# First attention of a two-layer gated cross-attention kernel: guard and copy dropped, query projection and output projection moved on TensorE

## What is computed

```
x = x + tanh(g_xattn[0]) * L0_xattn(layernorm(x), ctx, ctx)   # 16 heads of 16, 77 keys: the first attention
x = x + tanh(g_ffn[0])   * L0_ffn(layernorm(x))               # gelu(x @ patterns), mean, top-k, ...
x = x + tanh(g_xattn[1]) * L1_xattn(layernorm(x), ctx, ctx)   # with rotary positions and a mask
x = x + tanh(g_ffn[1])   * L1_ffn(layernorm(x))               # 16 experts and a shared one

L0_xattn:  q = x Wq^T + bq;  k, v likewise from ctx
           attn = softmax(-0.25 * q k^T);  out = (attn v) Wp^T + bp
```

## Time and profile before

| | |
|---|---|
| time, 3 runs | 737.0 us median (736.0 to 739.29) |
| the profiled execution | 738.46 us, its span 736.7 us |
| busy over the span | TensorE 655.6 us (89%), VectorE 454.4 (62%), ScalarE 353.8 (48%), GpSimd 237.6 (32%) |
| chain of work that ended last | TensorE 71%, VectorE 15%, issue 5%, DMA 3% |
| first attention | iteration 0 about 31 to 46 us, iterations 1 to 5 to 102 us, 6 and 7 to about 127 us |

### The profile page before, as it was taken

How to read it: one execution, slowest core, us unless ns; L and a number is a source line. 1 busy time by engine, 2 the same in 40 slices (tenths; PEclk the granted TensorE clock), 3 DMA queues, 4 the chain that set the end, 5 groups by cost and what they waited for, 6 DMA issues and landing times.

```text
span 736.7 us, 13204 instructions
## 1 busy us (share of the span) xinstructions
PE 655.6 (89%) x4816; PEld 534.0 (72%) x4816; DVE 454.4 (62%) x944; ACT 353.8 (48%) x780; POOL 237.6 (32%) x250
## 2 busy tenths in 40 slices
PE   4898988899988777766999979999888999999998
PEld 3676665778866455544566657999877999999997
DVE  3779877110117476767787636548896877778703
ACT  3267656656652233241657675233276565655400
POOL 6644522600000410036775312000134455555400
PEclk9899999999999989995999999999999999999999
DMA  7856650592000053005767642200002566666313
GB/s 260 266 159 159 184 149 1 214 420 83 0 0 1 15 205 106 7 1 133 143 157 138 144 68 85 88 2 1 1 0 86 178 210 204 203 203 203 114 29 114
DMA packets 61348, 87.17 MB, mean 118 GB/s; under 512 B 17257, under 2 KB 50665, under 8 KB 60265
## 3 DMA queue, kind: packets, MB, share of 16 engines
q1 hardware_dynamic: 60496, 85.90, 38.8%
q10 hardware_dynamic: 800, 0.59, 0.3%
HBM read 63.54 MB, written 18.73 MB: 112 GB/s over the span
## 4 chain that ended last, share of the span: by engine, by line
PE 71%; DVE 15%; issue 5%; DMA 3%; ACT 3%; POOL 2%; ACTq 0%; DVEq 0%; POOLq 0%
PE ps L1093 69%; DVE keep L2030 2%; DMA m_rows<-big 1%; DMA keep<-in_x 1%; DVE keep L2041 1%; PE ps L1099 1%; DVE keep L2038 1%; DVE keep L2023 1%; DVE G L2243 1%; ACT vp L768 1%; DVE mcol L1838 1%; DVE hhi_s L2170 1%; DVE att L2168 0%; ACT ps L889 0%; DVE keep L1852 0%
## 5 line engine op out<-in xcount | busy, mean ns | idle before, releaser
L1093 PE MATMUL ps<-keep 128*128 128x120 bf16 (+7 forms) x473 | 60.6, 257 | 20.0 <-DVE keep L2030 14.7
L1093 PE MATMUL ps<-thi,whi 128*128 128x256 f32 x256 | 73.6, 287 | 4.1 <-POOL tlo L698 2.1
L1093 PE MATMUL ps<-thi,wlo 128*128 128x256 f32 x256 | 72.3, 283 | 0.0
L1093 PE MATMUL ps<-tlo,whi 128*128 128x256 f32 x256 | 72.2, 282 | 0.0
L1093 PEld LDWEIGHTS ps<-keep 128*128 128x128 bf16 (+1 forms) x473 | 34.1, 112 | 41.2 <-DVE keep L2030 26.2
L889 ACT ACTIVATE ps<-ps 128x256 f32<-128x256 f32 x128 | 47.6, 372 | 33.8 <-PE ps L1093 33.7
L1001 ACT ACTIVATE att<-ps 128x512 f32<-128x512 f32 x48 | 28.6, 596 | 65.6 <-PE ps L1093 65.4
L562 POOL TENSOR_TENSOR kbr<-khi,keep 128x616 fp32r<-128x616 f32 x32 | 39.8, 1265 | 61.2 <-PE ps L1093 59.0
L1093 PE MATMUL ps<-xhi,phi 128*128 128x512 f32 x128 | 51.5, 402 | 5.3 <-ACT ps L889 2.9
L1093 PEld LDWEIGHTS ps<-thi,whi 128*128 128x128 f32 x256 | 48.6, 190 | 6.0 <-issue 3.6
L1093 PE MATMUL ps<-xhi,plo 128*128 128x512 f32 x128 | 50.6, 395 | 0.0
(11 more groups left out here) (250 smaller groups left out, 1854.9 us busy)
## 6 DMA issues: line engine op xcount, KB each, us to landing
q_rows<-qhi SPq DMA_DIRECT2D x32, 256.0 KB, 2.7
big<-in_piw SPq DMA_DIRECT2D x4, 2048.0 KB, 13.4
qpair<-q_rows SPq DMA_DIRECT2D x8, 768.0 KB, 5.7
qhead<-q_rows SPq DMA_DIRECT2D x8, 768.0 KB, 7.7
q_rows<-qlo SPq DMA_DIRECT2D x16, 256.0 KB, 2.9
att<-in_wg SPq DMA_DIRECT2D x8, 512.0 KB, 3.7
att<-in_wu SPq DMA_DIRECT2D x8, 512.0 KB, 4.6
att<-in_wd SPq DMA_DIRECT2D x8, 512.0 KB, 5.6
```

The costliest lines, as they stand in the source:

```text
L1093: return pe.matmul(out, lhsT, rhs, start=start, stop=stop, skip_group_check=True)
```

## The change

In the first attention:

- TensorE: the query projection of block n + 2 stands at the head of iteration n, ahead of the first key scores. Its first row scores follow behind these, then the output projection of block n - 1, and only then the second key scores. Second row scores come before the third key scores.
- ScalarE: the high queries are taken before the first exponentials, and the second normalisation moves from behind the third exponentials to before the second.
- VectorE: the guard is gone, and the reciprocal reads the denominators where they are. The second statistics move from behind to before the second half of the maxima.

In both attentions the aggregation writes `fmv` directly, without the copy, and GpSimd waits for the two aggregations. The counts of the semaphore within `divide` go from three steps to two.

```diff
@@ attend, ScalarE @@
+                    if n + 2 < hi and layer == 0:
+                        high_queries(n + 2)
                     exponentials(n, (0, 1))
                     if n == 2 * B - 1:
                         round_shared(0)
-                    if n + 2 < hi and layer == 0:
-                        high_queries(n + 2)
...
+                    if n >= 2 and layer == 0:
+                        normalise_second(n - 2)
                     exponentials(n, (2, 3))
...
-                    if n - 2 >= lo:
+                    if n - 2 >= lo and layer == 1:
                         normalise_second(n - 2)
@@ attend, TensorE @@
+                    if m < hi and layer == 0:
+                        project_q(m)
                     key_scores(n, (0, 1))
-                    if m < hi:
-                        if layer == 0:
-                            project_q(m)
-                        else:
-                            swap_pairs(m)
+                    if m < hi and layer == 1:
+                        swap_pairs(m)
...
+                    if layer == 0 and m < hi:
+                        if m >= 5:
+                            pe.wait_ge(xlo_done, m - 4)
+                        first_rows(m)
+                        if n > lo:
+                            project_out(n - 1)
                     key_scores(n, (2, 3))
                     if layer == 0 and m >= hi:
                         early_acts(m - hi, 1)
-                    if layer == 0:
-                        if m < hi:
-                            if m >= 5:
-                                pe.wait_ge(xlo_done, m - 4)
-                            first_rows(m)
-                    elif n + 3 < hi:
+                    if layer == 1 and n + 3 < hi:
                         scale_rows(n + 3)
...
+                    if m < hi and layer == 0:
+                        second_rows(m)
                     key_scores(n, (4, 5))
-                    if n > lo:
+                    if n > lo and (m >= hi or layer == 1):
                         project_out(n - 1)
-                    if m < hi:
-                        if layer == 0:
-                            second_rows(m)
-                        else:
-                            first_rows(m)
+                    if m < hi and layer == 1:
+                        first_rows(m)
@@ stats_second, VectorE @@
-                    dve.bn_aggr(fag[:, t, :], fbn[:, t, :]).then_inc(faggr_done, 1)
-                dve.wait_ge(faggr_done, k * 2 + 2)
-                dve.tensor_copy(fmv[:, tiles(b), :], fag).then_inc(fmv_done, 1)
+                    dve.bn_aggr(fmv[:, 2 * b + t, :], fbn[:, t, :]).then_inc(fmv_done, 1)
@@ divide, VectorE @@
-                dve.tensor_scalar(den, turned4[:, :, :, HD], TINY, None, ALU.max).then_inc(div_step, 1)
-                dve.wait_ge(div_step, 3 * i + 1)
-                dve.reciprocal(rec, den).then_inc(div_step, 1)
+                dve.reciprocal(rec, turned4[:, :, :, HD]).then_inc(div_step, 1)
@@ attend_first, VectorE @@
                     if n > 0:
                         add_projection(n - 1)
+                        stats_second(n - 1)
                     if n + 2 < B:
                         maxima(n + 2, 1)
-                    if n > 0:
-                        stats_second(n - 1)
                     divide(n, 0)
@@ inv_std_second, GpSimd @@
-                pool.wait_ge(fmv_done, k + 1)
+                pool.wait_ge(fmv_done, 2 * k + 2)
```

More of the change, by code:

```diff
@@ L111, in flamingo_kernel @@
         fbn = keep(2 * 6).rearrange("p (t k) -> p t k", k=6)
-        fag = keep(2 * 2).rearrange("p (t k) -> p t k", k=2)
         fmv = keep(T // P * 2).rearrange("p (t k) -> p t k", k=2)
@@ L125, in flamingo_kernel @@
         scaled = tk[:, 512:768]
-        den, rec = (tk[:, at:at + 16].rearrange("p (a t) -> p a t", a=2) for at in (768, 784))
+        rec = tk[:, 768:784].rearrange("p (a t) -> p a t", a=2)
         tied, above, above_lo, eqb = (keep(64).bitcast(BF16) for _ in range(4))
@@ L267, in flamingo_kernel @@
         cleared, prepared, tanh_done, bpt_done = sem("cleared"), sem("prepared"), sem("tanh_done"), sem("bpt_done")
-        fstat_done, faggr_done, fmv_done = sem("fstat_done"), sem("faggr_done"), sem("fmv_done")
+        fstat_done, fmv_done = sem("fstat_done"), sem("fmv_done")
         fveps_done, frstd_done = sem("fveps_done"), sem("frstd_done")
@@ L1845, in divide @@
                 if n >= B:
-                    dve.wait_ge(div_step, 3 * 2 * B + i - 2 * B + 1)
+                    dve.wait_ge(div_step, 2 * 2 * B + i - 2 * B + 1)
                     dve.wait_ge(proj_ps, n)
@@ L1853, in divide @@
                 dve.wait_ge(half_read, i + 1)
-                dve.tensor_scalar(den, turned4[:, :, :, HD], TINY, None, ALU.max).then_inc(div_step, 1)
-                dve.wait_ge(div_step, 3 * i + 1)
-                dve.reciprocal(rec, den).then_inc(div_step, 1)
-                dve.wait_ge(div_step, 3 * i + 2)
+                dve.reciprocal(rec, turned4[:, :, :, HD]).then_inc(div_step, 1)
+                dve.wait_ge(div_step, 2 * i + 1)
                 dve.tensor_tensor(scaled.rearrange("p (t a d) -> p a t d", a=2, d=HD), turned4[:, :, :, 0:HD],
                                   rec.unsqueeze(3).to_broadcast([P, 2, S // 32, HD]), ALU.mult).then_inc(div_step, 1)
-                dve.wait_ge(div_step, 3 * i + 3)
+                dve.wait_ge(div_step, 2 * i + 2)
                 if n > 0:
```

## The result

The changed kernel takes 734.4 us, the median of 20 runs (731.03 to 738.79), and the kernel before beside it 741.11 us, the median of 20 (735.27 to 746.78): ratio 0.9908, 95% interval 0.9884 to 0.9932. So the change saves some 0.6 to 0.9%, 4.5 to 6.8 us, where the forecast had 4.6 us. The forecast's 732.4 us started from three runs of before at 737.0; the twenty beside the changed kernel lie 4.1 us higher, which is why the time came out 2.0 us above the forecast although the gain is larger.

The account below looks back on a forecast made before the run. The prediction saw one loop through three engines, TensorE and VectorE about equally full, decided by who waits for whom. Terms 3.0 - 1.1 + 1.07 + 1.64 = 4.6 us gave profiled 733.8, median 732.4 us; range 729.0 to 736.3.

Parts of the forecast that it names:

- Step 1: Iteration 0: query projection fills TensorE's wait for the maxima and the clock stays at 2.4 GHz; gain 3.0 us.
- ScalarE's queue end: Iteration 0: ScalarE's queue ends later than TensorE's 42.0, so iteration 1 starts at 42.6 us.
- Step 2: Iterations 1 to 4: the new order takes 47.25 us against 46.17; loss 1.1 us.
- VectorE has slack here, and its 0.59 us is hidden: Iterations 1 to 4: the 0.59 us taken off VectorE saves nothing, being hidden by TensorE's two waits.
- VectorE was the real limit: Rival, iterations 1 to 4: VectorE sets the loop, some 11.3 us an iteration, gain 1.0, total 730.3 us; chance 0.15.
- delays the maxima: Iterations 1 to 4: statistics moved ahead delay the second maxima by 0.94 us, still ending at 9.05, before TensorE's 9.5.
- Step 3: Into iteration 6: the early pattern matmuls come 12.8 us after iteration 5's start, against 13.87; gain 1.07 us.
- Step 4: Iterations 6 and 7: clock stays up (1.05 us) and VectorE drops two guards and a copy; gain 1.64 us.
- the clock falls all the same: Rival: clock still falls at 30 and 105 us, leaving gain 2.3, 734.7 us, no measurable change; chance 0.20.
- The port: Rival, iterations 1 to 3: GpSimd's work meets VectorE's products on SBUF, 1.8 us lost, 734.2 us; chance 0.14.
- The guard at 81.83: Iteration 4: guard took 0.75 us instead of 0.17, ending with GpSimd's key blocks; taken as agreeing with the exclusion rule.
- Slower: Rival: clock falls inside the loop, about 3.2 us each time; three falls cost 9.6, total 742.0 us; chance 0.06.

Follow-up runs that it names:

- e12: The changed kernel, unchanged, run and profiled again beside the kernel before on one chip: 736.34 us, ratio to before 0.9940.
- e9: Kernel before without guard and copy on VectorE, second statistics moved ahead of the second maxima, other orders old: 739.85 us, ratio to before 0.9975.
- e8: Kernel before without guard and copy, iteration 0's query projection and high queries moved first, other orders old: 734.08 us, ratio to before 0.9904.
- e2: Changed kernel with guard and copy put back on VectorE, so the new orders alone: 741.05 us, ratio to before 1.0002.
- e4: Kernel before with only iteration 0's query projection and high queries moved first: 741.6 us, ratio to before 0.9988.
- e5: Changed kernel with the second key scores ahead of the output projection again: 736.72 us, ratio to before 0.9937.
- e6: e5 with ScalarE's normalisation of four blocks ahead moved before the second exponentials in iterations 1 to 3: 736.51 us, ratio to before 0.9950.
- e13: The program of e8, unchanged, run and profiled again: 735.40 us, ratio to before 0.9934.
- e10: e8 with VectorE splitting the pattern tile and making the low part before its first division in iteration 5: 731.06 us, ratio to before 0.9866.
- e11: The kernel before, unchanged, run and profiled again: 739.98 us, ratio to before 0.9987.
- e3: Changed kernel with iteration 0's query projection and high queries back in the old order: 735.88 us, ratio to before 0.9937.
- e1: Kernel before without guard and copy on VectorE, every order as before: 736.01 us against 742.48, ratio 0.9921.

## Why the prediction was right, step by step

The forecast was 4.6 us. By the stages the change saves 90.81 - 85.26 = 5.55 us, 5.61 in the second pair of profiles, and the runs, 4.5 and 6.8 us, lie around it. In the first pair 1.67 of this did not show at O, because A came late.

**Step 1, iteration 0: 3.0 forecast, 3.5 measured.** From A to the start of iteration 1 were 16.99 us (28.61 to 45.60) and are 13.48. e12 starts iteration 1 at 41.83, the forecast had 42.6. The forecast had ScalarE's queue end too late, and that was the mis-sized term: ScalarE does hold TensorE (0.74 us at 42.76), but the iteration still ended half a microsecond sooner than taken. The size hangs on the clock: e9, in the old order but at a clock of 1.00 from 30 to 37 us, takes 14.48 from A to P1, and e8, which has only the order of iteration 0 different up to there, 13.70. So without the fall the order is worth about 0.8. Over all profiles the clock stayed at 1.00 in iteration 0 in all nine with the query projection first (after, e12, e2, e4, e5, e6, e8, e13, e10) and fell in four of the five with the old order (before, e11, e3, e1, but not e9).

**Step 2, iterations 1 to 4: 1.1 lost by the forecast, 0.55 measured.** The output projection came 4.00 after the start (3.89), and the starts of e12 lie 11.49, 11.77, 11.75 and 11.69 apart (11.7, 11.95, 11.95 and 11.65): ScalarE's copy of the maxima holds the next projection up by 0.23 and not 0.3. The sign was right. Wrong was "VectorE has slack here, and its 0.59 us is hidden": the maxima were to end at 9.05, 0.45 ahead of TensorE's 9.5, and they end at 9.22, 0.07 ahead of the transposes at 9.29. With guard and copy back in, the loop takes 0.95 longer (e2, 47.67), because its maxima are then too late for the transposes. And the old loop was VectorE's, but for 0.69 us in which it waits for the output projection: without these 0.59 us it takes 43.85. The rival *VectorE was the real limit* was thus true of the kernel before, and false of the changed one, because the statistics ahead of the maxima (3.9 us by e9) give back more than VectorE had gained. The forecast saw that this "delays the maxima" and costed it at nothing.

**Step 3, into iteration 6: 1.07 forecast, 0.88 measured.** From the end of the maxima to the pattern matmul it is 3.77 us (3.75 forecast), but the maxima end 9.22 after the start and not 9.05. The gap shrank from 2.43 to 0.91 us as forecast.

**Step 4: 1.64 forecast, 1.71 measured (13.78 to 12.07).** Both parts came as forecast. From E to the addition at 108.06 are 4.59 us, 1.15 less than before (1.05 forecast), and from there to O 7.48, 0.56 less (0.59 forecast). That the first part is the clock show e8 and e13, one program: with the fall it takes 5.99 us (100.55 to 106.54), without it 4.59 (98.88 to 103.47), and the rest up to O is 7.46 in both.

The rivals: *the clock falls all the same* came true in e2 behind a gap of 1.60 us (E to O 13.96) but in neither profile of the changed kernel. *The port* came in part: five products took longer than 0.5 us (0.54 to 0.82), and soon after four of them VectorE stood 0.72 to 0.83 us waiting for another engine, so they cost the loop nothing. The fifth, at 100.64, lies in the chain to the pattern matmul and took 0.66 us where before's took 0.43. GpSimd's work beside the longest, the product at 77.20:

```profile
76.52 1.23 POOL L561 TENSOR_TENSOR kbr<-khi,keep 128x616 fp32r<-128x616 f32 x1
77.70 1.41 POOL L561 TENSOR_TENSOR kbr<-khi,keep 128x616 fp32r<-128x616 f32 x1
```

The first ended at 77.75 and the product at 78.02, 0.27 behind it; the second took 1.41 us where these instructions take 1.22 in the median, so both engines slowed. The Trainium skill (SBUF — State Buffer, "two separate sides") has the two exclude each other for a whole instruction. The rows agree with that: the product ended only behind GpSimd's first, and GpSimd's second was the one that got longer. The guard at 81.83, which the forecast counted as agreeing, reads one tile only and is no test of the rule as the forecast put it. *Slower* did not come: the clock was 1.00 from 44 to 100 us.

So the gain came out right for mostly the right reasons, with one of them upside down. By the stages the dropped steps alone give 4.2 us (e1, in a profile without the fall behind E) and the order of iteration 0 alone 3.9 (e4); both together give 8.3 (e13), and the rest of the new order takes 2.7 of that back. The forecast had the steps worth nothing in the loop and everything there down to TensorE's waits. The total did not suffer from that, because the forecast added up the new loop as a whole and not the two halves of the change.

## What to carry to other kernels

When a loop runs through several engines, take each dropped instruction out alone: a saving that the new order hides may be the full pace of the old one. Ahead of a result that another engine waits for, put nothing that nobody waits for; one group of statistics in front of the maxima cost 1 us in every iteration. Judge changes of under 1% by stages between fixed points of the trace, and where the stages and the whole time disagree, as for e4, e10 and e13, say so.

## What was not expected of the hardware

The whole time of one program moves by over 1% with the granted clock (735.28 to 745.46 us for before). Yet in both profiles of one program most falls stand at the same places, and a few do not. Behind O, e11 falls where before does and once more, 415 us behind O. The two profiles of the changed kernel agree up to 235 us behind O, and e12 then falls at three places more, 240, 325 and 450 us behind O. The second of these, first in the changed kernel's first profile, then in e12:

```profile
440.50:445.50 5.00, 5.00 (x75) 3.12 (x73) 3.27 (x9) 2.74 (x6) 2.13 (x4) 1.00 0.00 0
438.50:443.50 5.00, 4.49 (x13) 3.50 (x14) 1.22 (x1) 3.94 (x7) 0.00 (x0) 0.50 0.00 0
```

A gap in TensorE's work ahead of the first pattern matmul of 2.43 us had a fall behind it three times out of three (before, e11, e4), 2.06 us once in three (e8, but not e1 and e13), 1.60 us in the one profile that has it (e2; so had the 1.49 us of e10 at the output projection), 1.31 us once in three (e9, but not e5 and e6), and 0.9 us in none of three (after, e12, e3). In iteration 0 a gap of 1.38 to 1.40 us had one three times out of three (before, e11, e3) and 2.89 us in e1, but 1.31 (e9) and 1.32 us (e2) had none. So a short wait costs its own length and, by chance, 1.4 us more (e8 against e13).

Left untried: the changed kernel's order on TensorE with the maxima ahead of the statistics on VectorE, which by e9 should be the shortest loop, and longer series of e10 and e13, which could settle their last 0.3%.
